# Group ends of the scan: state keys turned behind the second output part, last parts signalled tile by tile, masks moved up

## Chip, cores and metric

The kernel runs on one core of a Trainium2 chip. The metric is the device time of one execution in microseconds. Five engines with queues of their own take part: TensorE (PE, its weight loads PEld), VectorE (DVE), ScalarE (ACT), GpSimd (POOL) and SyncE (SP, which issues the DMAs). They are ordered among each other by semaphores only: an instruction that waits holds up all that stands behind it in its engine's queue.

## What is computed

Six blocks with residual connections work on 1024 tokens (two sequences of 512) of width 512: a gated feed-forward block, a state-space mixer, the feed-forward block again, a routed block, an attention block, and the routed block again. The change is in the mixer. Cut to what matters:

```
proj = rmsnorm(x) @ in_proj_w.T            # gate 8192, hid 8192, B and C 8 x 128 each, dt 128 heads
hid, B, C = silu(causal_conv(hBC))         # 4 taps
M = (C @ B.T) * exp(segsum(A dt))          # inside a chunk, lower triangle
y = M @ (hid dt)  +  C @ state carried from the chunk before  +  Dp * hid
yg = y * silu(gate)
out = rmsnorm over each of 8 groups of 1024 (yg) * gnorm_w @ out_proj_w.T
x = x + out
```

Each of the 8 groups has its own B and C, which its 16 heads share.

## The kernel before

`mamba` (line 1237 on) handles the mixer as a scan over 64 units of two heads (128 columns). Eight units form a group (GT = 8), and there are 8 groups. All large products are done in three passes with operands split into a high and a low part: `matmul3` (lines 73 to 78) issues lo x hi, hi x hi and hi x lo into the same PSUM bank. The high part of a weight tile is made by ScalarE (`split`, L1574), the low part by GpSimd (`low`, L1710).

In a unit TensorE does, in the order of its queue: `states` (L1463, the state of the first chunk, bank 4), `within` for both sequences (L1478 and L1482, banks 5 and 6), `carried` (L1494, bank 7), the transposes of the next unit's hidden columns (`turn`, L1451), and the projections of a later hidden tile and a gate tile into pairs of banks 0 to 3. VectorE does the outputs of these (`skip`, `carried`, `by_token`), the convolution (L1795), the decay differences (L1812) and the `products` of decay and inner products (L1827).

After the eighth unit of a group comes its end, which is where the change lies:

- TensorE projects B and C of the next group, then does the output projection of the group: two output parts p (one for each sequence), each over i = 0 to 7 (`out_part`, called part (p,i) below). A part (p,i) is twelve products: four token tiles t, each accumulated over i in its own bank 4 + t, three passes each. Behind part (0,2) stand the sums of squares (`sums`, L1504). Between part (0,7) and part (1,0) stand the `inner` products of the next group (C B^T for both sequences, L1430 and L1432) and `turn_b` (L1441), which transposes the state keys B of the next group.
- ScalarE makes the high part of the scaled operand (`z_part`, L1646) two parts ahead, and after each part splits the weight tile four ahead (`after_part`). `turned_b` (L1592) copies the transposed keys out of PSUM, ahead of its work for the parts (1,i).
- VectorE makes the operand's low part (`z_low`, L1854), one for each part; after part (p,7) it adds the four finished tiles to x (`outputs`, L1867), each scaled by the reciprocal root of the group's mean square. Between the low parts of sequence 1 it also masks the next group's inner products (`masked`, L1818) and does the products of the next unit (L1827).
- GpSimd makes the low parts of the weights, one for each part, and `rstd` (L1781) behind one of them.

Banks 0 to 3 are two pairs that the users take in turn in the order of `Plan.uses`. A user waits until the one two places ahead in that list has been read: the transposed keys ("bt") share a pair with the inner products of sequence 0 ("cb", grp, 0), so `turn_b` waits for the mask of that sequence; the states of the next unit 8, 16, ... wait for the copied keys and for the first of the four outputs of sequence 1, as bank 4 is used again.

One semaphore `out_used` counts parts; it is raised by the last product of each part. Readers wait for part number + 1: `z_part` before it overwrites an operand buffer, `after_part` before it overwrites a weight buffer, `outputs` once, for part (p,7), before all four tiles.

Of the kernel before, what the change touches and what calls it, by code (L numbers as in the profile page):

```python
# [35 lines left out]
GT = GW // P  # L36
# [1200 lines left out]
def mamba(nc, g, name):  # L1237
# [7 lines left out]
    with ExitStack() as ctx:  # L1245
# [17 lines left out]
        with ExitStack() as pre:  # L1263
# [24 lines left out]

        names = ("const_in", "cw_in", "full", "w_hi", "w_lo", "tapped", "active", "hc_ready", "hcw_ready", "sub_d",
                 "sub_a", "sub_p", "exped", "m_ready", "state", "prev_ready", "y_done", "o_done", "skipped", "yo_ready",  # L1290
                 "combined", "gated", "squared", "added", "rstd_ready", "z_hi", "z_lo", "out_used", "out_read", "dve")
        s = {n: c_.sem(n) for n in names}
        free = [c_.sem(f"free{i}") for i in range(2)]
        raw_in = [c_.sem(f"raw_in{i}") for i in range(NRAW)]
# [26 lines left out]

        def part(grp, p, i):
            return (grp * 2 + p) * GT + i

        with nc.Block() as block:
            @block.sync
# [77 lines left out]
            def _(e):  # L1404
# [103 lines left out]
                def out_part(grp, p, i):  # L1508
                    k, q = plan.tile["o", grp, p, i], part(grp, p, i)
                    e.wait_ge(s["w_lo"], k + 1)  # L1510
                    e.wait_ge(s["z_lo"], q + 1)
                    if i == 0 and p == 0:
                        e.wait_ge(s["skipped"], (grp + 1) * GT)
                        e.wait_ge(s["yo_ready"], (grp + 1) * GT)
                    for t in range(4):
                        if i == 0 and p == 1:
                            e.wait_ge(s["out_read"], 8 * grp + t + 1)
                        sl = (slice(None), q % 2, slice(t * P, (t + 1) * P))
                        last = matmul3(e, ps[4 + t], zs.hi[sl], zs.lo[sl], w.hi[:, k % NSPLIT, :],
                                       w.lo[:, k % NSPLIT, :], i == 0, i == GT - 1)  # L1520
                    last.then_inc(s["out_used"], 1)

                for item in (("B", 0), ("C", 0), ("h", 0), ("h", 1), ("g", 0)):
                    project(item, 0)
# [5 lines left out]
                for u in range(UNITS):  # L1530
                    grp = u // GT
                    more = grp + 1 < GROUPS
                    states(u)
                    within(u, 0)
                    within(u, 1)
                    carried(u)
                    if u + 1 < UNITS:
                        turn(u + 1)
                    for item in (("h", u + 2), ("g", u + 1)):
                        if item[1] < UNITS:  # L1540
                            project(item, 0)
                            project(item, 1)
                    if u % GT < GT - 1:
                        continue
                    if more:
                        for item in (("B", grp + 1), ("C", grp + 1)):
                            project(item, 0)
                            project(item, 1)
                    for i in range(GT):
                        out_part(grp, 0, i)  # L1550
                        if i == 2:
                            sums(grp)
                    if more:
                        inner(grp + 1, 0)
                        inner(grp + 1, 1)
                        turn_b(grp + 1)
                    for i in range(GT):
                        out_part(grp, 1, i)

            @block.scalar  # L1560
            def _(e):
# [79 lines left out]
                def z_part(grp, p, i):  # L1641
                    q = part(grp, p, i)
                    e.wait_ge(s["gated"], grp * GT + i + 1)
                    if q >= 2:
                        e.wait_ge(s["out_used"], q - 1)
                    e.activation(zs.hi[:, q % 2, :], z[:, i, p, :], ACT.Copy, scale=dgn[:, grp, i, 1:2]  # L1646
                                 ).then_inc(s["z_hi"], 1)

                def after_part(grp, p, i):
                    e.wait_ge(s["out_used"], part(grp, p, i) + 1)  # L1650
                    split(plan.tile["o", grp, p, i] + 4)

                for k in range(4):
# [12 lines left out]
                for u in range(UNITS):  # L1666
                    grp, i = divmod(u, GT)
                    more = grp + 1 < GROUPS
                    if u + 1 < UNITS:
                        silu("h", u + 1)  # L1670
                    pass_states(u)
                    if i:
                        gate_silu(u)
                    if u + 1 < UNITS:
                        decay(2 * u + 2)
                        all_differences(2 * u + 3)
                    if u + 2 < UNITS:
                        newest_tap("h", u + 2)
                    if u + 1 < UNITS:
                        decay(2 * u + 3)  # L1680
                    square(u)
                    if i < GT - 1:
                        continue
                    if more:
                        gate_silu(u + 1)
                    z_part(grp, 0, 0)
                    z_part(grp, 0, 1)
                    if more:
                        newest_tap("B", grp + 1)
                        newest_tap("C", grp + 1)  # L1690
                        silu("B", grp + 1)
                    for i in range(GT):
                        z_part(grp, (i + 2) // GT, (i + 2) % GT)
                        after_part(grp, 0, i)
                        if i == 2 and more:
                            silu("C", grp + 1)
                    if more:
                        turned_b(grp + 1)
                    for i in range(GT):
                        if i + 2 < GT:  # L1700
                            z_part(grp, 1, i + 2)
                        after_part(grp, 1, i)

            @block.gpsimd
            def _(e):
# [78 lines left out]
            def _(e):  # L1784
# [75 lines left out]
                                    ).then_inc(free[pair_of("sum", grp)], 1)  # L1860

                def outputs(grp, p):
                    e.wait_ge(s["out_used"], part(grp, p, GT - 1) + 1)
                    e.wait_ge(s["rstd_ready"], grp + 1)
                    for t in range(4):
                        n = p * 4 + t
                        e.scalar_tensor_tensor(x[:, n, :], ps[4 + t], rstd[:, n:n + 1], x[:, n, :], ALU.mult, ALU.add  # L1867
                                               ).then_inc(s["out_read"], 1)

# [12 lines left out]
                for u in range(UNITS):  # L1882
                    grp, i = divmod(u, GT)
# [27 lines left out]
                    z_low(grp, 1, 1)  # L1911
                    if more:
                        masked(grp + 1, 0)
                    z_low(grp, 1, 2)
                    if more:
                        products(2 * u + 2)
                    z_low(grp, 1, 3)
                    if more:
                        masked(grp + 1, 1)
                    z_low(grp, 1, 4)  # L1920
                    if more:
                        products(2 * u + 3)
                    for i in range(5, GT):
                        z_low(grp, 1, i)
                    outputs(grp, 1)

# [243 lines left out]
```

## Time and profile before

| what | value |
|---|---|
| median of 3 runs | 2625.44 us (2620.22 to 2627.13) |
| the profiled execution | 2624.77 us |
| its span | 2622.7 us |
| mean granted TensorE clock | 0.959 |
| PE busy | 2382.1 us, 91% |
| DVE busy | 1674.2 us, 64% |
| ACT busy | 1315.6 us, 50% |
| POOL busy | 1336.2 us, 51% |

A busy share is taken over the whole span. The scan of the mixer takes from about 300 to 1925 us of it. The hardware's records give the start of an instruction well; the end of a matmul is modelled, and neighbouring matmuls overlap in the records, so distances between starts are the better measure on TensorE. On VectorE an instruction's record overlaps the one before it by some 0.1 us. A clock of 1.00 is 2.4 GHz, 0.50 is 1.2 GHz.

### The profile page before, as it was taken

The numbers are of one execution on the slowest core, as the hardware profiler recorded it, in microseconds if no ns is written. First come the engines' busy times: TensorE is split into PE (matmuls) and PEld (weight loads), VectorE is DVE, ScalarE is ACT, GpSimd is POOL, SyncE is SP. The second block draws the span as 40 slices with busy tenths as digits, with TensorE's granted clock in tenths as the row PEclk, the third lists the DMA queues.
The fourth block names the chain that finished last, engine by engine and source line by source line (L and its number), as shares of the span: only waits on it lengthen the run. The fifth ranks groups of instructions, "written<-read, shape, count | busy, mean of one in ns | idle before, by whom it ended". The sixth has DMA issues, their size and how long they took to land. (4 is left out here: it accounts for less than half of the span.)

```text
span 2622.7 us, 32589 instructions
## 1 busy us (share of the span) xinstructions
PE 2382.1 (91%) x12122; PEld 1839.7 (70%) x12122; DVE 1674.2 (64%) x2174; ACT 1315.6 (50%) x1910; POOL 1336.2 (51%) x881
## 2 busy tenths in 40 slices
PE   4995689999999999999999999999759987989986
PEld 4874468778778778878878878878648763565643
DVE  4554478578678678678678678668445534574424
ACT  2321367557557557557657657657423214325533
POOL 1222169669669669759759759759612210000000
PEclk9997799999999999999999999999879997989998
DMA  3430323323323323323323323323114312000001
GB/s 99 107 87 1 95 89 113 96 89 113 97 89 110 97 88 112 96 86 113 97 86 106 103 79 107 109 77 113 52 48 107 96 27 75 1 2 2 2 2 45
DMA packets 163260, 203.97 MB, mean 78 GB/s; under 512 B 24380, under 2 KB 86080, under 8 KB 162976
## 3 DMA queue, kind: packets, MB, share of 16 engines
q1 hardware_dynamic: 163104, 201.90, 26.1%
q8 instruction: 97, 1.59, 0.3%
q14 instruction: 59, 0.48, 0.1%
HBM read 198.37 MB, written 3.15 MB: 77 GB/s over the span
## 5 line engine op out<-in xcount | busy, mean ns | idle before, releaser
L1710 POOL TENSOR_TENSOR mamba_w_lo<-mamba_raw,mamba_w_hi 128x512 fp32r<-128x512 f32 x272 | 435.3, 1610 | 292.8 <-ACT mamba_w_hi L1574 292.8
L76 PE MATMUL psum<-mamba_hT_lo,mamba_w_hi 128*128 128x512 f32 x1152 | 461.7, 401 | 6.5 <-POOL mamba_w_lo L1710 6.5
L78 PE MATMUL psum<-mamba_hT_hi,mamba_w_lo 128*128 128x512 f32 x1152 | 456.0, 396 | 0.0
L77 PE MATMUL psum<-mamba_hT_hi,mamba_w_hi 128*128 128x512 f32 x1152 | 455.9, 396 | 0.0
L1729 POOL TENSOR_SCALAR mamba_L<-mamba_A,mamba_ts 128x256 f32<-128x256 f32 (+1 forms) x256 | 333.3, 1317 | 0.1
L1827 DVE TENSOR_TENSOR mamba_L<-mamba_L,mamba_cb 128x1536 f32<-128x1536 f32 x128 | 309.0, 2414 | 22.5 <-ACT mamba_L L1623 14.2
L1795 DVE SCALAR_TENSOR_TENSOR mamba_hid<-psum,mamba_cw,mamba_hid 128x1022 f32<-128x1022 f32 (+2 forms) x192 | 245.1, 1277 | 21.4 <-ACT mamba_hid L1581 16.8
L76 PEld LDWEIGHTS psum<-mamba_hT_lo,mamba_w_hi 128*128 128x128 f32 x1152 | 216.9, 188 | 56.6 <-POOL mamba_w_lo L1710 6.7
L78 PEld LDWEIGHTS psum<-mamba_hT_hi,mamba_w_lo 128*128 128x128 f32 x1152 | 216.7, 188 | 52.4
L77 PEld LDWEIGHTS psum<-mamba_hT_hi,mamba_w_hi 128*128 128x128 f32 x1152 | 217.1, 188 | 49.1
L350 POOL TENSOR_TENSOR ffn_w_lo<-ffn_deq,ffn_w_hi 128x512 fp32r<-128x512 f32 (+2 forms) x66 | 84.4, 1279 | 296.0 <-ACT ffn_w_hi L360 296.0
L1854 DVE SCALAR_TENSOR_TENSOR mamba_zs_lo<-mamba_z,mamba_dgn,mamba_zs_hi 128x512 fp32r<-128x512 f32 x128 | 117.2, 920 | 175.2 <-ACT mamba_zs_hi L1646 175.2
L1812 DVE SCALAR_TENSOR_TENSOR mamba_L<-mamba_A,mamba_ts,mamba_zero 128x256 f32<-128x256 f32 (+1 forms) x512 | 215.7, 489 | 10.8 <-DMA mamba_A<-mamba_a_dram 10.8
L76 PE MATMUL psum<-mamba_w_lo,mamba_zs_hi 128*128 128x512 f32 x512 | 205.7, 402 | 14.0 <-DVE mamba_zs_lo L1854 13.1
L77 PE MATMUL psum<-mamba_w_hi,mamba_zs_hi 128*128 128x512 f32 x512 | 203.4, 397 | 0.0
L78 PE MATMUL psum<-mamba_w_hi,mamba_zs_lo 128*128 128x512 f32 x512 | 203.3, 397 | 0.0
L1646 ACT ACTIVATE mamba_zs_hi<-mamba_z,mamba_dgn 128x512 fp32r<-128x512 f32 x128 | 91.7, 722 | 192.0 <-PE psum L78 192.0
L1574 ACT CAST mamba_w_hi<-mamba_raw 128x512 fp32r<-128x512 f32 x272 | 165.9, 610 | 36.5 <-PE psum L78 25.8
L489 POOL MEMSET routed_qT<- 1x1024 f32 x2 | 1.9, 945 | 356.3 <-POOLq L53 356.3
L1581 ACT ACTIVATE mamba_hid<-psum,mamba_cw 128x1024 f32<-128x1024 f32 x64 | 77.2, 1206 | 202.0 <-PE psum L78 202.0
L1478 PE MATMUL psum<-mamba_L,mamba_hc 128*64 128x256 f32 x1024 | 159.6, 390 | 3.7 <-DVE mamba_L L1827 3.7
L76 PE MATMUL psum<-ffn_hT_lo,ffn_w_hi 128*128 128x512 f32 (+1 forms) x352 | 139.4, 396 | 23.3 <-POOL ffn_w_lo L350 23.3
(284 smaller groups left out, 4975.1 us busy)
## 6 DMA issues: line engine op xcount, KB each, us to landing
mamba_A<-mamba_a_dram SPq DMA_DIRECT2D x128, 512.0 KB, 4.5
mamba_raw<-in_win SPq DMA_DIRECT2D x144, 256.0 KB, 2.7
mamba_raw<-in_wout SPq DMA_DIRECT2D x128, 256.0 KB, 2.6
mamba_Eb<-mamba_e_dram SPq DMA_DIRECT2D x128, 128.0 KB, 3.0
ffn_raw<-in_w SPq DMA_DIRECT2D x80, 128.0 KB, 3.5
ffn_scl<-in_s SPq DMA_DIRECT2D x80, 128.0 KB, 3.7
ffn_scl<-in_s SPq DMA_DIRECT2D x86, 64.0 KB, 2.4
ffn_raw<-in_w SPq DMA_DIRECT2D x20, 256.0 KB, 2.7
```

The lines of the kernel that those rows point to most:

```text
L76: e.matmul(out, wh, ml, start=start, stop=False)
L77: e.matmul(out, wh, mh, start=False, stop=False)
L78: return e.matmul(out, wl, mh, start=False, stop=stop)
L1478: e.matmul(psum[lo:lo + HD, 5 + b, q:q + HALF], hc[:, token_tile(b, c, 0), lo:lo + HD], L[:, m % 3, c, h, 0:HALF], start=True, stop=False)
L1574: e.copy(w.hi[:, k % NSPLIT, :], raw[:, k % NRAW, :]).then_inc(s["w_hi"], 1)
L1646: e.activation(zs.hi[:, q % 2, :], z[:, i, p, :], ACT.Copy, scale=dgn[:, grp, i, 1:2]).then_inc(s["z_hi"], 1)
L1710: e.tensor_tensor(w.lo[:, k % NSPLIT, :], raw[:, k % NRAW, :], w.hi_read[:, k % NSPLIT, :], ALU.subtract).then_inc(s["w_lo"], 1)
L1729: last = e.tensor_scalar(out, A[:, m % 2, h, lo:SEQ], ts[:, token_tile(b, 1, j), 1, head], 0.0, ALU.subtract, ALU.min)
L1795: ins = e.scalar_tensor_tensor(t[:, :, k:], banks(kind, n)[:, :, :SEQ - k], cw[:, grp, i, 3 - k:4 - k], t[:, :, k:], ALU.mult, ALU.add)
L1812: last = e.scalar_tensor_tensor(out, A[:, m % 2, h, lo:hi], ts[:, token_tile(b, c, j), 1, head], zero[:, 0:1].to_broadcast([P, hi - lo]), ...
L1827: e.tensor_tensor(t, t, cb[:, m % 2].unsqueeze(2).to_broadcast([P, 2, 2, WCOL]), ALU.mult).then_inc(s["m_ready"], 1)
L1854: e.scalar_tensor_tensor(zs.lo[:, q % 2, :], z[:, i, p, :], dgn[:, grp, i, 1:2], zs.hi_read[:, q % 2, :], ALU.mult, ALU.subtract).then_inc ...
```

## The change

- `turn_b` of the next group leaves its place ahead of part (1,0) and stands behind part (1,1); ScalarE's `turned_b` likewise stands behind its work for part (1,1).
- The last part of each sequence, (p,7), raises a new semaphore `out_done` four times, once for each finished token tile, and no longer `out_used`, which now counts seven parts for each sequence. A function `taken` gives for a part number the semaphore and the value to wait for. `outputs` waits for each tile by itself instead of once for all four.
- VectorE's order behind part (0,7): before it was low part (1,1), mask 0, low part (1,2), products of the next unit's sequence 0, low part (1,3), mask 1, low part (1,4), products of its sequence 1, low parts (1,5) to (1,7). Now it is low part (1,1), mask 0, products of sequence 0, mask 1, low part (1,2), products of sequence 1, low parts (1,3) to (1,7).

```diff
--- before.py
+++ after.py
@@ -1288,7 +1288,7 @@
 
         names = ("const_in", "cw_in", "full", "w_hi", "w_lo", "tapped", "active", "hc_ready", "hcw_ready", "sub_d",
                  "sub_a", "sub_p", "exped", "m_ready", "state", "prev_ready", "y_done", "o_done", "skipped", "yo_ready",
-                 "combined", "gated", "squared", "added", "rstd_ready", "z_hi", "z_lo", "out_used", "out_read", "dve")
+                 "combined", "gated", "squared", "added", "rstd_ready", "z_hi", "z_lo", "out_used", "out_done", "out_read", "dve")
         s = {n: c_.sem(n) for n in names}
         free = [c_.sem(f"free{i}") for i in range(2)]
         raw_in = [c_.sem(f"raw_in{i}") for i in range(NRAW)]
@@ -1321,6 +1321,11 @@
 
         def part(grp, p, i):
             return (grp * 2 + p) * GT + i
+
+        def taken(q):
+
+            n, i = divmod(q, GT)
+            return (s["out_done"], 4 * (n + 1)) if i == GT - 1 else (s["out_used"], n * (GT - 1) + i + 1)
 
         with nc.Block() as block:
             @block.sync
@@ -1518,7 +1523,10 @@
                         sl = (slice(None), q % 2, slice(t * P, (t + 1) * P))
                         last = matmul3(e, ps[4 + t], zs.hi[sl], zs.lo[sl], w.hi[:, k % NSPLIT, :],
                                        w.lo[:, k % NSPLIT, :], i == 0, i == GT - 1)
-                    last.then_inc(s["out_used"], 1)
+                        if i == GT - 1:
+                            last.then_inc(s["out_done"], 1)
+                    if i < GT - 1:
+                        last.then_inc(s["out_used"], 1)
 
                 for item in (("B", 0), ("C", 0), ("h", 0), ("h", 1), ("g", 0)):
                     project(item, 0)
@@ -1553,9 +1561,10 @@
                     if more:
                         inner(grp + 1, 0)
                         inner(grp + 1, 1)
-                        turn_b(grp + 1)
                     for i in range(GT):
                         out_part(grp, 1, i)
+                        if more and i == 1:
+                            turn_b(grp + 1)
 
             @block.scalar
             def _(e):
@@ -1642,12 +1651,12 @@
                     q = part(grp, p, i)
                     e.wait_ge(s["gated"], grp * GT + i + 1)
                     if q >= 2:
-                        e.wait_ge(s["out_used"], q - 1)
+                        e.wait_ge(*taken(q - 2))
                     e.activation(zs.hi[:, q % 2, :], z[:, i, p, :], ACT.Copy, scale=dgn[:, grp, i, 1:2]
                                  ).then_inc(s["z_hi"], 1)
 
                 def after_part(grp, p, i):
-                    e.wait_ge(s["out_used"], part(grp, p, i) + 1)
+                    e.wait_ge(*taken(part(grp, p, i)))
                     split(plan.tile["o", grp, p, i] + 4)
 
                 for k in range(4):
@@ -1694,12 +1703,12 @@
                         after_part(grp, 0, i)
                         if i == 2 and more:
                             silu("C", grp + 1)
-                    if more:
-                        turned_b(grp + 1)
                     for i in range(GT):
                         if i + 2 < GT:
                             z_part(grp, 1, i + 2)
                         after_part(grp, 1, i)
+                        if more and i == 1:
+                            turned_b(grp + 1)
 
             @block.gpsimd
             def _(e):
@@ -1860,10 +1869,10 @@
                                     ).then_inc(free[pair_of("sum", grp)], 1)
 
                 def outputs(grp, p):
-                    e.wait_ge(s["out_used"], part(grp, p, GT - 1) + 1)
                     e.wait_ge(s["rstd_ready"], grp + 1)
                     for t in range(4):
                         n = p * 4 + t
+                        e.wait_ge(s["out_done"], 8 * grp + n + 1)
                         e.scalar_tensor_tensor(x[:, n, :], ps[4 + t], rstd[:, n:n + 1], x[:, n, :], ALU.mult, ALU.add
                                                ).then_inc(s["out_read"], 1)
 
@@ -1911,16 +1920,13 @@
                     z_low(grp, 1, 1)
                     if more:
                         masked(grp + 1, 0)
+                    if more:
+                        products(2 * u + 2)
+                        masked(grp + 1, 1)
                     z_low(grp, 1, 2)
                     if more:
-                        products(2 * u + 2)
-                    z_low(grp, 1, 3)
-                    if more:
-                        masked(grp + 1, 1)
-                    z_low(grp, 1, 4)
-                    if more:
                         products(2 * u + 3)
-                    for i in range(5, GT):
+                    for i in range(3, GT):
                         z_low(grp, 1, i)
                     outputs(grp, 1)
```

## Rows read from the trace of the kernel before

**Rows 1.** Cores: span and mean granted TensorE clock.
```profile
core 0: 2622.7 us, clock 0.959
```

**Rows 2.** Windows: length, busy time of PE, PEld, DVE, ACT, POOL, clock, DMA.
```profile
343.00:510.00 167.00, 166.94 (x939) 135.13 (x940) 129.63 (x141) 114.11 (x148) 139.34 (x88) 0.99 0.35 106
510.00:546.00 36.00, 32.70 (x153) 26.03 (x153) 19.94 (x21) 13.96 (x24) 16.26 (x12) 1.00 0.28 81
```

**Rows 3.** Waits of TensorE: in total, times, the longest.
```profile
PE psum L76 <- DVE mamba_zs_lo L1854: 13.1, 8, 8.7
...
PE psum L1441 <- DVE mamba_cb L1818: 12.1, 7, 1.7
...
PE psum L1463 <- DVE s_x L1867: 6.5, 7, 0.9
```

**Rows 4.** Timeline, TensorE: start, length, instruction, idle before; ahead of part (1,0).
```profile
517.40 0.38 PE L1432 MATMUL psum<-mamba_bc 128*128 128x128 f32 x2
519.51 0.66 PE L1441 MATMUL psum<-s_ident,mamba_bc 128*128 128x128 f32 x4 [1.73 <-DVE mamba_cb L1818]
519.92 0.51 PE L76 MATMUL psum<-mamba_w_lo,mamba_zs_hi 128*128 128x512 f32 x1
```

**Rows 5.** Timeline, VectorE, first group end.
```profile
515.21 2.73 DVE L1867 SCALAR_TENSOR_TENSOR s_x<-psum,mamba_rstd,s_x 128x512 f32<-128x512 f32 x4 [1.23 <-PE psum L78]
517.85 0.74 DVE L1854 SCALAR_TENSOR_TENSOR mamba_zs_lo<-mamba_z,mamba_dgn,mamba_zs_hi 128x512 fp32r<-128x512 f32 x1
518.51 0.95 DVE L1818 TENSOR_TENSOR mamba_cb<-psum,mamba_mask 128x768 f32<-128x768 f32 x1
...
524.52 2.85 DVE L1827 TENSOR_TENSOR mamba_L<-mamba_L,mamba_cb 128x1536 f32<-128x1536 f32 x1
527.30 1.79 DVE L1854 SCALAR_TENSOR_TENSOR mamba_zs_lo<-mamba_z,mamba_dgn,mamba_zs_hi 128x512 fp32r<-128x512 f32 x1
```

**Rows 6.** Timeline, TensorE, from part (1,2) to part (1,3).
```profile
528.21 0.39 PE L78 MATMUL psum<-mamba_w_hi,mamba_zs_lo 128*128 128x512 f32 x1
529.24 0.47 PE L76 MATMUL psum<-mamba_w_lo,mamba_zs_hi 128*128 128x512 f32 x1 [0.64 <-DVE mamba_zs_lo L1854]
```

**Rows 7.** Timeline, TensorE: end of part (1,7), and the next unit.
```profile
543.08 0.40 PE L78 MATMUL psum<-mamba_w_hi,mamba_zs_lo 128*128 128x512 f32 x1
544.41 1.13 PE L1463 MATMUL psum<-mamba_hcw,mamba_bt 128*128 128x128 f32 x8 [0.94 <-DVE s_x L1867]
...
547.90 0.39 PE L1482 MATMUL psum<-mamba_L,mamba_hc 128*64 128x128 f32 x4
548.22 1.13 PE L1494 MATMUL psum<-mamba_bc,mamba_prev 128*128 128x256 f32 x4
...
561.03 0.40 PE L78 MATMUL psum<-mamba_hT_hi,mamba_w_lo 128*128 128x512 f32 x1
561.26 0.94 PE L1463 MATMUL psum<-mamba_hcw,mamba_bt 128*128 128x128 f32 x7
```

**Rows 8.** Timeline, GpSimd, first group end.
```profile
516.57 1.27 POOL L1710 TENSOR_TENSOR mamba_w_lo<-mamba_raw,mamba_w_hi 128x512 fp32r<-128x512 f32 x1 [1.45 <-ACT mamba_w_hi L1574]
524.41 1.35 POOL L1710 TENSOR_TENSOR mamba_w_lo<-mamba_raw,mamba_w_hi 128x512 fp32r<-128x512 f32 x1 [6.56 <-ACT mamba_w_hi L1574]
```

**Rows 9.** Lines of products and low parts: shortest, median, longest in ns.
```profile
L1827 DVE TENSOR_TENSOR mamba_L<-mamba_L,mamba_cb x128: 1757/2404/3018, 336.3 to 1854.4; 128x1536 f32<-128x1536 f32 x128
...
L1854 DVE SCALAR_TENSOR_TENSOR mamba_zs_lo<-mamba_z,mamba_dgn,mamba_zs_hi x128: 735/751/2346, 482.2 to 1917.0; 128x512 fp32r<-128x512 f32 x128
```

**Rows 10.** Timeline, ScalarE: high part of (1,2).
```profile
523.10 0.72 ACT L1646 ACTIVATE mamba_zs_hi<-mamba_z,mamba_dgn 128x512 fp32r<-128x512 f32 x1 [2.31 <-PE psum L78]
```

**Rows 11.** Timeline, TensorE and VectorE, end of the last group.
```profile
1899.04 0.47 PE L76 MATMUL psum<-mamba_w_lo,mamba_zs_hi 128*128 128x512 f32 x1 [0.94 <-DVE s_x L1867]
...
1921.72 2.73 DVE L1867 SCALAR_TENSOR_TENSOR s_x<-psum,mamba_rstd,s_x 128x512 f32<-128x512 f32 x4 [4.01 <-PE psum L78]
1925.45 4.85 DVE L137 BATCH_NORM_STATS2 ffn_n_st<-s_x 128x6 f32<-128x512 f32 x8 [1.00 <-PEq L53]
```

## The prediction

> **What bounds the kernel now.** I read the totals first, then the table of who waited for whom, then three stretches of the timeline around the end of one group of the scan. The profiled execution has a span of 2622.7 us [rows 1] and took 2624.77 us, so 2.07 us lie outside the span; it stands 0.67 us under the median of the runs, 2625.44 us. The table by stretches shows what sets the pace in the scan: from 343 to 510 us TensorE is busy for 166.94 of 167.00 us at a granted clock of 0.99, that is at its 2.4 GHz level, while VectorE has 129.63 and GpSimd 139.34; from 510 to 546, the end of the first group, TensorE has only 32.70 of 36 [rows 2]. So between group ends nothing but TensorE counts, and each microsecond in which it stands still at a group end is a microsecond of the kernel. The table of waits names what stops it there: the mask (L1818) before the transposes of the state keys, 12.1 us in seven times; the output of the gated sum (L1867) before the states, 6.5 in seven; the low part of the output operand (L1854), 13.1 in eight, of which one is an 8.7 us wait at the last group that this change does not touch, so seven share about 4.4 [rows 3]. That is (12.1 + 6.5 + 4.4) / 7 = 3.3 us idle for each of the seven group ends that have a successor.
>
> **Where the three stops lie (first group end).** I measure from start to start, since the modelled ends of matmuls overlap by some 0.17 us.
> A: the last inner product starts at 517.40, the transposes at 519.51, the first product of output part (1,0) at 519.92: 2.52 us [rows 4]. The transposes cannot start before the mask of sequence 0 has freed their two PSUM banks, and VectorE does that mask only after four outputs (2.73 us) and a low part [rows 5].
> B: the last product of part (1,2) starts at 528.21, the first of part (1,3) at 529.24 [rows 6]. The pitch of such products is 0.23 (561.03 to 561.26 [rows 7]), so 0.80 is lost. VectorE had put products (2.85 us) between the low parts of (1,2) and (1,3), and the latter itself took 1.79 [rows 5].
> C: the last product of part (1,7) starts at 543.08, the states at 544.41, 1.33 us later; one unit on, where nothing stands between, it is 561.03 to 561.26, 0.23 [rows 7]. So 1.10 is lost waiting for the first of four outputs, which starts only when all four tiles of the part are finished.
>
> **The change, part by part.**
> *Transposes behind part (1,1), their copy in ScalarE's queue likewise.* TensorE goes from the inner products to part (1,0) without asking for a mask. The switch costs something like the one from L1482 to L1494, 547.90 to 548.22, 0.32 us [rows 7]. A shrinks from 2.52 to 0.32: part (1,0) starts 2.20 earlier, at S = 517.72. The other conditions of that part are met: its low operand is written at 513.98 (VectorE's idle time of 1.23 before the outputs at 515.21 begins there [rows 5]), and its first tile needs only the first output. The bounds of the switch are 0.23 (no cost beyond the pitch) and 0.41 (519.51 to 519.92, in which four transposes go by as well [rows 4]); I take 0.32, since it too goes from 128-column products to wider ones. The four transposes are not removed: in the new place they cost 519.92 - 519.51 = 0.41, and the restart after them 0.12 (by the stretch 519.92 to 528.21, 36 products at 0.23 and 0.2 over), 0.53 in all. What ScalarE's copy of the 512 columns delays there: the queue behind it is the high part of (1,4), which waits for the end of part (1,2) anyway, over 2 us later; the weights of (1,1) are split before it. It also no longer holds ScalarE ahead of part (1,2). Nothing is taken from or given to SP's queue, and GpSimd's order is the same; the weight loads follow the parts.
> *Masks and products moved up.* This decides whether B goes. I lay VectorE's new order out against the rows. Part (0,7) still ends at 515.21; its tiles of three products (0.70 us each) are finished at 513.11, 513.81, 514.51 and 515.21. VectorE is free at 513.98, so the four outputs run with their present pitch of 2.64 / 4 = 0.66 and the next instruction starts at 516.62 instead of 517.85. Then low part (1,1) to 517.28, mask 0 to 518.23, products(16) with up to 2.85 to 521.1, mask 1 to 522.0. If GpSimd is idle, which it is from 517.84 until the split after part (1,0) [rows 8], products(16) take their shortest 1.76 [rows 9], and the second mask ends at 520.9. Low part (1,2) needs its high part, which follows the end of part (1,0): 523.10 - 519.92 + 0.72 = 3.90 after S [rows 4, 10], that is 521.62. So VectorE is back in time, the low part runs to 522.4, and part (1,2) wants it at S + 2 x 2.84 + 0.53 = 523.93 (2.84 is a part: (528.21 + 0.23 - 519.92) / 3). From here the distances to S are those of before: products start at S + 4.60, beside the same GpSimd split, and part (1,3) can start at 529.24 - 519.92 = S + 9.32. TensorE asks for it at S + 8.52 + 0.53 = S + 9.05. So the stall B is not removed by the move: its 0.80 is filled with the transposes, and 0.27 remains. A and B together give exactly the 2.20 by which S comes earlier, with bounds of 2.11 (the switch at its dear end) and 2.29 + 0.27 = 2.56 (cheap switch, no stall left). Behind (1,3) VectorE has only low parts left, so it is not late again.
> *Last parts signal tile by tile.* In part (1,7) the first tile is finished 2.10 before the last, VectorE has nothing else to do (4.01 idle ahead of the same outputs in the last group [rows 11]), and the first output of 0.74 is over 1.2 us before the states want bank 4. The second, third and fourth end at most 0.74 after the last tile, while the carried product asks for the fourth 3.8 us after the states begin (548.22 - 544.41 [rows 7]). C falls to 0.23: 1.10 saved; bounds 0 and 1.10. In the last group the same wait stands before part (1,0) (0.94 idle at 1899.04 [rows 11]) and goes for the same reason: 1.10. At the very end the four outputs start at 1921.72 and take 2.73, and the statistics of the next stage follow them after 1.00 [rows 11]; with tiles signalled singly only the fourth is left behind the last product: 2.73 - 0.74 = 1.99 saved, all on the path, because TensorE waits for VectorE there.
> *Signals.* Sixteen last parts carry four signals instead of one, and VectorE four waits instead of one. The row bound is zero: the last product of a projection, at 561.03, carries a signal too, and the next one starts the plain 0.23 behind it [rows 7]. The Trainium skill, page "TensorE: Matmul & The Clock Gate", section "The cost: per-tile semaphore tail", speaks against this change: increments on completion serialize at about 26 ns each. By that rule 48 more increments are an estimated 1.2 us; the sum would be 25.0 instead of 26.2. No run here shows it, and I do not count it.
> *The shared port.* That a low part or a products instruction stretches beside a GpSimd subtraction is in the rows: products take 2.85 against a shortest 1.76, with GpSimd's 1.35 us instruction started 0.11 before them [rows 5, 8, 9]; the outputs, which read PSUM, run at 0.74 each through the whole of GpSimd's 516.57 instruction. No row has a mask beside GpSimd; I take it like an output, as it also reads PSUM, with 1.29 (a whole GpSimd instruction) as the other end, of which the 0.7 us between 520.9 and 521.62 takes half and the rest is the first rival's way. The Trainium skill, page "SBUF — State Buffer", section "Who interferes with whom", has this as an exclusive lock; by its rule for one SBUF input the mask would not be held, which leaves the sum as it is.
>
> **Sum.** 7 x 2.20 + 7 x 1.10 + 1.10 + 1.99 = 15.4 + 7.7 + 1.1 + 2.0 = 26.2 us. Against the profiled execution 2624.8 - 26.2 = 2598.6; against the median 2599.2. I say 2599.
>
> **Rivals.**
> 1. *VectorE is late for low part (1,2) by one lock.* Products(16), low part (1,1) or a mask meet GpSimd's subtraction at 516.57 or take 2.85 rather than 1.76, the whole row slides, and products(17) start later. If VectorE gains nothing from the single signals (low part (1,1) at 517.85 and mask 0 at 518.51 as today), low part (1,2) starts at 518.51 + 0.95 + 2.85 + 0.95 less the small overlaps of neighbours, about 523.1 instead of 521.66, and part (1,3) slides by the same 1.45: 7 x 1.45 = 10.2 given back, 2609. For it: low part (1,1) at 516.62 and GpSimd at 516.57 nearly coincide. Against it: one such meeting costs at most 1.3, and between 520.9 and 521.62 only the rest counts.
> 2. *The states stay held.* Another condition, the rest of the outputs or ScalarE's queue, replaces C: 7.7 lost, 2607. Against: the distances of 1.2 and 3.8 us above.
> 3. *Slower than before.* The moved masks and products now stand before low part (1,2), and if each meeting with GpSimd is at its dearest, TensorE waits twice. With the longest low part of the trace, 2.35, and the longest products, 3.02 [rows 9]: 516.62 + 2.35 + 0.95 + 3.02 + 0.95 + 2.35 = 526.2; then 3.02 + 2.35 more, and part (1,3) starts at 531.8, S + 14.0 instead of S + 9.3. That is 4.7 a group against 3.3 saved: +1.4 x 7 - 3.1 = +6.7, 2632. It decides from S + 13.1 on. Against it: the extreme rows come from elsewhere in the scan (here products are 2.85 at most), and GpSimd has but one instruction for each part.
> 4. *The signals do not do what they say*, because TensorE's tiles finish no earlier than the part does for VectorE: C and the end stay, 15.4 is left, 2610.
>
> **Chances.** Forecast 0.75, first rival 0.12, second 0.04, fourth 0.03, slower 0.03, the rest 0.03. The range goes from the full 2.56 a group and some of the spread of the runs below their median (26.2 + 2.5 + 4 off 2625.4) to the first rival: 2593 to 2610. What a measurement can tell is 0.3%, 7.9 us: faster than 2617.6 0.93, within 0.04, slower 0.03; all rivals but the third are faster by more.
>
> **What would show it.** No wait of L1441 for the mask; L1463 without a wait for L1867 at seven places; the step from the last inner product to part (1,0) near 0.3; transposes of 0.4 inside part (1,1)'s end; a wait of at most 0.3 for L1854 at part (1,3); the period from one group's transposes to the next 3.3 us shorter; VectorE's last output ending one output behind TensorE. I am wrong if L76 waits longer than 1 us for L1854 in a group, if a wait for anything new stands before L1463, or if the units between group ends, now with no idle time, get longer.

## The result and the profile after

The changed kernel takes 2591.28 us (median of 4 runs, 2589.62 to 2592.27) against 2625.72 (4 runs, 2620.22 to 2627.13): a ratio of 0.9869, 95% interval 0.9854 to 0.9883, or 34.4 us less. Forecast were 26.2 us and 2599, with a range that ended at 2593.

TensorE's waits in the changed kernel, that answer to [rows 3]:

```profile
PE psum L76 <- DVE mamba_zs_lo L1863: 10.0, 8, 8.7
...
PE psum L1468 <- ACT mamba_bt L1601: 5.7, 1, 5.7
```

Line numbers are 5 to 9 higher than before (the states are L1468, the transposes L1446, the low part L1863, the outputs L1876). The mask and the outputs are gone from the list. Of the 10.0 us for low parts, 8.7 are the last group's, unchanged, and seven waits share 1.3. The wait for the copied keys is the one at the very start of the scan.

TensorE's timeline at the first group end (start, length, instruction, idle before), that answers to [rows 4, 6, 7] (a row with x2 or x4 stands for so many instructions in a row, with the start of the first):

```profile
521.29 0.38 PE L1437 MATMUL psum<-mamba_bc 128*128 128x128 f32 x2
521.43 0.48 PE L76 MATMUL psum<-mamba_w_lo,mamba_zs_hi 128*128 128x512 f32 x1
521.75 0.39 PE L77 MATMUL psum<-mamba_w_hi,mamba_zs_hi 128*128 128x512 f32 x1
521.98 0.39 PE L78 MATMUL psum<-mamba_w_hi,mamba_zs_lo 128*128 128x512 f32 x1
...
526.88 0.40 PE L78 MATMUL psum<-mamba_w_hi,mamba_zs_lo 128*128 128x512 f32 x1
527.12 0.60 PE L1446 MATMUL psum<-s_ident,mamba_bc 128*128 128x128 f32 x4
527.48 0.48 PE L76 MATMUL psum<-mamba_w_lo,mamba_zs_hi 128*128 128x512 f32 x1
...
530.12 0.39 PE L78 MATMUL psum<-mamba_w_hi,mamba_zs_lo 128*128 128x512 f32 x1
530.70 0.47 PE L76 MATMUL psum<-mamba_w_lo,mamba_zs_hi 128*128 128x512 f32 x1 [0.19 <-DVE mamba_zs_lo L1863]
...
544.55 0.39 PE L78 MATMUL psum<-mamba_w_hi,mamba_zs_lo 128*128 128x512 f32 x1
544.78 1.05 PE L1468 MATMUL psum<-mamba_hcw,mamba_bt 128*128 128x128 f32 x8
```

From the start of the last two inner products to part (1,0) it is 0.14 us instead of 2.52. The transposes take 0.36 at their new place behind part (1,1), and the product behind them is followed by the next 0.31 us later instead of 0.23: 0.44 in all. Part (1,3) begins 9.27 us after part (1,0), against 9.32 before: still held by the low part, for 0.35 beyond the pitch (0.58 from start to start) instead of 0.80. The states follow part (1,7) at the plain pitch of 0.23. The other six group ends repeat these distances within 0.02 us.

VectorE over the same stretch, that answers to [rows 5]:

```profile
517.78 2.72 DVE L1876 SCALAR_TENSOR_TENSOR s_x<-psum,mamba_rstd,s_x 128x512 f32<-128x512 f32 x4
520.41 0.74 DVE L1863 SCALAR_TENSOR_TENSOR mamba_zs_lo<-mamba_z,mamba_dgn,mamba_zs_hi 128x512 fp32r<-128x512 f32 x1
521.07 0.95 DVE L1827 TENSOR_TENSOR mamba_cb<-psum,mamba_mask 128x768 f32<-128x768 f32 x1
522.13 1.79 DVE L1836 TENSOR_TENSOR mamba_L<-mamba_L,mamba_cb 128x1536 f32<-128x1536 f32 x1
523.84 0.94 DVE L1827 TENSOR_TENSOR mamba_cb<-psum,mamba_mask 128x768 f32<-128x768 f32 x1
525.34 0.75 DVE L1863 SCALAR_TENSOR_TENSOR mamba_zs_lo<-mamba_z,mamba_dgn,mamba_zs_hi 128x512 fp32r<-128x512 f32 x1 [0.55 <-ACT mamba_zs_hi L1655]
526.00 2.85 DVE L1836 TENSOR_TENSOR mamba_L<-mamba_L,mamba_cb 128x1536 f32<-128x1536 f32 x1
528.77 1.78 DVE L1863 SCALAR_TENSOR_TENSOR mamba_zs_lo<-mamba_z,mamba_dgn,mamba_zs_hi 128x512 fp32r<-128x512 f32 x1
```

and GpSimd beside it, that answers to [rows 8]:

```profile
520.46 1.84 POOL L1719 TENSOR_TENSOR mamba_w_lo<-mamba_raw,mamba_w_hi 128x512 fp32r<-128x512 f32 x1 [1.45 <-ACT mamba_w_hi L1583]
525.88 1.35 POOL L1719 TENSOR_TENSOR mamba_w_lo<-mamba_raw,mamba_w_hi 128x512 fp32r<-128x512 f32 x1 [3.58 <-ACT mamba_w_hi L1583]
528.69 1.31 POOL L1719 TENSOR_TENSOR mamba_w_lo<-mamba_raw,mamba_w_hi 128x512 fp32r<-128x512 f32 x1 [1.46 <-ACT mamba_w_hi L1583]
```

The outputs run straight behind low part (1,0), VectorE is back 0.55 us before low part (1,2) can start, and then the old pattern returns: products of 2.85 behind GpSimd's instruction at 525.88, low part (1,3) of 1.78 behind the one at 528.69.

**Where the 34.4 us are.** To see what belongs to the group ends and what does not, I cut every trace at five starts of TensorE: the inner products of sequence 1 for the first group (335.36 us in the kernel before), the last unit's states (1851.45), the scan's last product (1921.28), the first transpose of the next stage (1933.53) and the program's last product (2612.46). "Step" is the stretch from the third to the fourth, "behind" that from the fourth to the fifth. In us, one profiled execution each, and the median of the timed runs:

```
kernel            start   7 group ends'  last    step to     behind   median
                  at      part of scan   group   next stage
before            335.4   1516.1         69.8    12.25       678.9    2625.7
before, again     339.2   1515.8         69.9    12.24       673.5    2623.1
masks alone       336.0   1516.5         68.2    12.23       672.3    2625.1
turn alone        335.8   1499.7         70.0    12.23       675.3    2606.9
turn and masks    336.1   1503.2         69.7    12.24       675.0    2610.9
signals alone     335.3   1498.4         68.8    10.26       678.9    2601.5
turn and signals  335.5   1491.3         67.5    10.26       678.1    2592.5
changed           339.3   1491.2         67.1    10.26       672.1    2591.3
changed, again    337.8   1490.9         67.3    10.26       672.2    2592.0
end at once       335.3   1490.9         68.3    12.30       672.2    2598.6
shift by two      335.9   1491.0         67.2    11.57       676.5    2593.9
shift by four     336.9   1490.6         66.9    12.89       678.3    2599.1
products later    338.7   1488.0         66.9    10.27       671.9    2588.3
```

The second column repeats within 0.4 us for one kernel. The change takes 24.9 us there (forecast 23.1), 2.7 in the last group (1.1), 1.99 in the step (1.99): 29.6 us. The other 4.8 of 34.4 come from no stretch in which a line was changed. In the profiled pair such stretches give 3.0: 6.9 less behind the scan, 3.9 lost ahead of it (the start at 335.4 or 339.2 in the two profiles of the kernel before, 339.3 and 337.8 in those of the changed one). The last 1.9 are the difference between the medians, 34.4, and the profiled executions, 2624.8 - 2592.3 = 32.5. A profiled execution can lie well off its median (masks alone 2618.7, end at once 2591.8), so what an edit does is read from the columns by stretch, and the medians only confirm it.

### The profile page after: what moved, and what is told of

Same layout as the page of the kernel before. It is cut to its first block and busy times, and to the rows that moved or that the text cites. A ratio compares the mean times of both kernels' runs of the same rounds, so it can differ in the third digit from the quotient of the medians.

```text
span 2590.2 us, 32589 instructions
## 1 busy us (share of the span) xinstructions
PE 2371.8 (92%) x12122; PEld 1835.4 (71%) x12122; DVE 1668.5 (64%) x2174; ACT 1314.4 (51%) x1910; POOL 1336.1 (52%) x881
## 5 line engine op out<-in xcount | busy, mean ns | idle before, releaser
L1836 DVE TENSOR_TENSOR mamba_L<-mamba_L,mamba_cb 128x1536 f32<-128x1536 f32 x128 | 301.9, 2359 | 23.1 <-ACT mamba_L L1632 14.2
L1863 DVE SCALAR_TENSOR_TENSOR mamba_zs_lo<-mamba_z,mamba_dgn,mamba_zs_hi 128x512 fp32r<-128x512 f32 x128 | 117.5, 923 | 171.8 <-ACT mamba_zs_hi L1655 171.8
```

What stands on the lines that cost most here:

```text
L1836: e.tensor_tensor(t, t, cb[:, m % 2].unsqueeze(2).to_broadcast([P, 2, 2, WCOL]), ALU.mult).then_inc(s["m_ready"], 1)
L1863: e.scalar_tensor_tensor(zs.lo[:, q % 2, :], z[:, i, p, :], dgn[:, grp, i, 1:2], zs.hi_read[:, q % 2, :], ALU.mult, ALU.subtract).then_inc ...
```

## The experiments

**1. The changed kernel again**, no edit.

> The changed kernel once more, nothing edited. Theory: the scan gives the same 27 to 28 us in every execution (24.9 at the seven group ends, about 3 at the last), and what the profiled pair shows outside the scan (4.4 us lost ahead of it, 8.8 won behind it) is where TensorE's half-rate stretches happen to fall; then the distance from the last group's end to the end of the program differs from the 714.0 us of the first profile of this kernel by 1 us or more, and the ratio stays within 0.985 to 0.990. Rival: the 8.8 us behind the scan belong to the change; then that distance repeats within 0.5 us and lies 8 to 9 us below that of every profile of the kernel before.

Measured: 2592.02 us (2591.24 to 2592.13), ratio 0.9884 [0.9868, 0.9899]. The stretch behind the scan is 672.2, so the rival's first half held: it repeats.

**2. The kernel before again**, no edit.

> The kernel before once more, nothing edited. Theory (half-rate stretches fall differently from run to run): its stretch behind the scan moves by more than 1 us against its own first profile, and total half-rate time is not 219 us again. Rival (the 8.8 us belong to the change): it repeats within 0.5 us. Ratio 1.000 within 0.002 under both.

Measured: 2623.08 us (2617.65 to 2628.64, 11 runs), ratio 1.0004 [0.9994, 1.0015]. Behind the scan 673.5 instead of 678.9: here the theory held. So neither was wholly right: this stretch takes 672 to 673.5 in some executions of either kernel, and 679 in one of the old.

**3. The transposes alone** behind part (1,1).

```diff
                         inner(grp + 1, 1)
-                        turn_b(grp + 1)
                     for i in range(GT):
                         out_part(grp, 1, i)
+                        if more and i == 1:
+                            turn_b(grp + 1)
...
-                    if more:
-                        turned_b(grp + 1)
                     for i in range(GT):
                         if i + 2 < GT:
                             z_part(grp, 1, i + 2)
                         after_part(grp, 1, i)
+                        if more and i == 1:
+                            turned_b(grp + 1)
```

> Only the transposes and their copy behind part (1,1); signals and VectorE's order as before. Theory: part (1,0) starts 0.14 behind the last inner product instead of 2.52, part (1,3) is held to its old distance of 9.3 from there, so 7 x 2.38 = 16.7 us, about 2609, and the 1.33 before the states stays. Rival (masks in their old place reach the transposes too late): TensorE waits for the mask behind part (1,1) and under 10 us are saved.

Measured: 2606.89 us (2598.61 to 2610.73), ratio 0.9938 [0.9920, 0.9957]. The seven group ends give 16.4 us (2.3 each); the waits of L1463 for the outputs stay at 6.6 us in seven. As the theory had it.

**4. The signals alone**: the new semaphore, `taken` and the wait for each tile, orders as before.

> Only the tile-by-tile signals; transposes and VectorE's order as before. Theory: the four outputs end 1.2 us earlier, so the mask does too and the wait before the transposes falls from 1.73 to about 0.5; with 1.10 before the states 7 x 2.3 + 1.1 + 2.0 = 19.2 us, about 2606. Together with the transposes alone this is more than the whole change, by the 7 x 1.2 that both save at the same wait. Rival (each edit saves waits of its own): only 7 x 1.1 + 3.1 = 10.8 us, about 2615.

Measured: 2601.45 us (2595.26 to 2606.23), ratio 0.9919 [0.9901, 0.9936]. The seven ends give 17.7 us, 2.5 each against the 2.3 expected, so the theory held and its rival (1.1 each) did not. This is the line in which the signals' hidden share stands, the mask's wait before the transposes (12.1 us before):

```profile
PE psum L1446 <- DVE mamba_cb L1826: 2.9, 7, 0.4
```

Single signals let VectorE reach the mask 1.3 us sooner. Alone, transposes and signals give 16.4 + 17.7 = 34.1, together (experiment 7) 24.8: at seven ends 9.3 us are the same wait, counted twice.

**5. VectorE's order alone.**

```diff
                         masked(grp + 1, 0)
+                    if more:
+                        products(2 * u + 2)
+                        masked(grp + 1, 1)
                     z_low(grp, 1, 2)
                     if more:
-                        products(2 * u + 2)
-                    z_low(grp, 1, 3)
-                    if more:
-                        masked(grp + 1, 1)
-                    z_low(grp, 1, 4)
-                    if more:
                         products(2 * u + 3)
-                    for i in range(5, GT):
+                    for i in range(3, GT):
                         z_low(grp, 1, i)
```

> Only VectorE's new order of masks and products; transposes and signals as before. Theory: mask 0 stays where it is, so the wait before the transposes stays at 1.73, and low part (1,2) is still followed by products, so the 0.62 before part (1,3) stays too: no change, 2624. Rival (it is the moved masks that fill the stall before (1,3)): 7 x 0.8 = 5.6 us less, 2618.

Measured: 2625.14 us (2618.09 to 2628.41, 12 runs), ratio 0.9997 [0.9984, 1.0009]. No change, and none at the seven ends (1516.5 against 1516.1 and 1515.8).

**6. Transposes and order, no signals.**

> The whole change without the tile-by-tile signals. Theory: low part (1,1) starts 1.2 later, so the second mask ends at about S + 4.5 and low part (1,2) meets GpSimd's split there; products and low part (1,3) slide, part (1,3) starts about 0.7 us later than with the transposes alone: 2607 + 5 = 2612 (this is the first rival of the prediction, in the kernel where VectorE gains nothing from the signals). Rival (the new order is at least harmless): 2607 or less, like the transposes alone.

Measured: 2610.86 us (2608.24 to 2613.99), ratio 0.9952 [0.9937, 0.9967]; the seven ends are 3.5 us longer than with the transposes alone. VectorE in this kernel, then GpSimd:

```profile
522.21 0.95 DVE L1819 TENSOR_TENSOR mamba_cb<-psum,mamba_mask 128x768 f32<-128x768 f32 x1
523.08 1.72 DVE L1855 SCALAR_TENSOR_TENSOR mamba_zs_lo<-mamba_z,mamba_dgn,mamba_zs_hi 128x512 fp32r<-128x512 f32 x1
524.72 1.75 DVE L1828 TENSOR_TENSOR mamba_L<-mamba_L,mamba_cb 128x1536 f32<-128x1536 f32 x1
526.39 1.77 DVE L1855 SCALAR_TENSOR_TENSOR mamba_zs_lo<-mamba_z,mamba_dgn,mamba_zs_hi 128x512 fp32r<-128x512 f32 x1
```

```profile
522.97 1.28 POOL L1711 TENSOR_TENSOR mamba_w_lo<-mamba_raw,mamba_w_hi 128x512 fp32r<-128x512 f32 x1 [4.14 <-ACT mamba_w_hi L1575]
525.77 1.84 POOL L1711 TENSOR_TENSOR mamba_w_lo<-mamba_raw,mamba_w_hi 128x512 fp32r<-128x512 f32 x1 [1.52 <-ACT mamba_w_hi L1575]
```

Here the second mask ends too late, GpSimd starts 0.11 us before low part (1,2), which takes 1.72 instead of 0.75, and everything behind it slides (part (1,2) begins 6.43 us behind part (1,0) instead of 6.05, part (1,3) 9.80 instead of 9.27): the first rival, at a third of the price I gave it (0.5 us a group, not 1.45), because the products then run free at 1.75.

**7. Transposes and signals, VectorE's order as before.**

> The whole change with VectorE's order as before. Theory: everything that was gained comes from the transposes and the signals; low part (1,2), products, low part (1,3) follow each other as in the kernel before, 9.3 us after S: scan 1558 us, time 2591 to 2593, the same as the whole change. Rival (the moved masks and products pay): 3 us or more above it.

Measured: 2592.49 us (2589.39 to 2595.0), ratio 0.9880 [0.9864, 0.9897]; the seven ends 1491.3 against 1491.2 for the whole change. Beside the other two edits, the moved masks and products give nothing.

**8. The changed kernel with the second products behind low part (1,3).**

```diff
                     z_low(grp, 1, 2)
+                    z_low(grp, 1, 3)
                     if more:
                         products(2 * u + 3)
-                    for i in range(3, GT):
+                    for i in range(4, GT):
```

> The changed kernel with the second products instruction moved from behind low part (1,2) to behind low part (1,3). Theory: low part (1,3) is ready before TensorE asks, the 0.35 us at part (1,3) (0.58 from start to start against 0.23) goes at seven ends: scan 2.4 us shorter than 1558.2, time 2589; products then end before low part (1,4) is wanted. Rival (the stall moves): products and GpSimd's split stand before low part (1,4), TensorE waits there for 0.4 or more, no gain or 2593.

Measured: 2588.28 us (2586.56 to 2589.04), ratio 0.9864 [0.9846, 0.9881]; every run of it is below every run of the changed kernel. The seven ends are 3.1 us shorter, a little more than the 7 x 0.35 expected: each gives 0.35 at the stop and 0.07 behind it, since part (1,3), when it begins after a stop, takes 2.87 or 2.88 us and otherwise 2.80. VectorE, with both low parts at 0.75 now:

```profile
524.68 0.75 DVE L1863 SCALAR_TENSOR_TENSOR mamba_zs_lo<-mamba_z,mamba_dgn,mamba_zs_hi 128x512 fp32r<-128x512 f32 x1 [0.55 <-ACT mamba_zs_hi L1655]
527.49 0.75 DVE L1863 SCALAR_TENSOR_TENSOR mamba_zs_lo<-mamba_z,mamba_dgn,mamba_zs_hi 128x512 fp32r<-128x512 f32 x1 [2.05 <-ACT mamba_zs_hi L1655]
528.15 2.85 DVE L1836 TENSOR_TENSOR mamba_L<-mamba_L,mamba_cb 128x1536 f32<-128x1536 f32 x1
530.93 0.74 DVE L1863 SCALAR_TENSOR_TENSOR mamba_zs_lo<-mamba_z,mamba_dgn,mamba_zs_hi 128x512 fp32r<-128x512 f32 x1
```

The one wait of TensorE left for a low part is the last group's. This is the best version found.

**9. The last group's outputs at once**: `outputs` waits for `out_done` at 8 x 7 + 4p + 4 first when the group is the last.

> The changed kernel, but in the last group both outputs wait until all four tiles are finished, as before the change. Theory: only the last group and the step behind it grow, by 1.1 (the wait before part (1,0), 0.94 idle) and 2.0 (10.26 to 12.25 us from the scan's last product to the next stage's first): 3.1 us on the 1591.3 or so of scan and step; of the time 2 to 9 us, since the stretch behind it can fall into either of the lengths seen, 672 or 675 to 679. Rival (the step is set by something else than the last outputs): 0.

Measured: the step is 12.30 instead of 10.26 and the last group 68.3 instead of 67.2, 3.1 us as the theory had it; the time is 2598.61 us (2591.77 to 2601.34), ratio 0.9896 [0.9878, 0.9914]. That is 6.6 to 7.3 over the changed kernel's medians, in the expected 2 to 9; but this run and the next two were timed on another chip than experiment 1, where the kernel before stood at 2626.3 beside them against 2623.7 beside experiment 1. By the ratios it is 3.1 us over experiment 1 and 7.1 over the first measurement. The profiled execution was the fastest of its runs.

**10 and 11. A pure delay behind the scan**: two or four more low parts behind the last outputs, written to the unused gate buffer.

```diff
                     outputs(grp, 1)
+                    if not more:
+                        for k in range(2):      # or 4
+                            e.scalar_tensor_tensor(gate[:, k // 2, k % 2, :], z[:, 0, 0, :], ...)
```

> The changed kernel with two more low parts (VectorE, 0.66 us each from start to start, into a buffer that nobody reads) behind the last outputs of the scan: a pure delay of 1.3 us between the scan and the stretch behind it. Theory (where TensorE's half-rate stretches fall depends on the moment at which the stages behind the scan begin): the stretch behind the scan changes its length by more than 1 us, so the time moves by clearly more or less than 1.3. Rival (its length belongs to the kernel's edits): 672.2 again and 1.3 us more in the time, 2593.

> As above with four, a pure delay of 2.6 us. Theory: the stretch behind the scan has another length than 672.2, by 1 us or more; the time lies anywhere from 2590 to 2601. Rival: 672.2 again, and 2594.5.

Measured: 2593.85 us (2589.16 to 2594.52), ratio 0.9878 [0.9860, 0.9897], and 2599.06 us (2595.53 to 2599.71), ratio 0.9901 [0.9885, 0.9916]. The steps are 11.57 and 12.89, the delays 1.3 and 2.6 as meant; behind them 676.5 and 678.3 instead of 672.2. The rival's 672.2 did not come in either profile. The times are weaker evidence than the profiles: the median of the shorter delay, 2593.9, cannot tell the two apart, and the longer one stands 7 to 8 us over the changed kernel's medians, but only 4.5 over experiment 1 by the ratios, whose intervals overlap.

## Why the prediction was wrong

The direction, the places and the order of the terms held; the sum was 8.2 us short, which put the time 1.7 us under the range. By the prediction's own steps:

- *A and the transposes.* "I take 0.32" for the switch from the inner products to part (1,0) was the wrong row: it measured 0.14, below even the bound of 0.23 "no cost beyond the pitch". Measured like the 2.52, from the start of the last two inner products, these 0.14 hold 0.11 from the one to the other and 0.03 to part (1,0), where the first pitch is then 0.32 (521.43 to 521.75) instead of 0.23. S, the start of part (1,0), came 2.38 earlier, not 2.20. The transposes and their restart cost 0.44 of the 0.53 given.
- *B.* As laid out: the stall is not removed but filled; 9.27 us from part (1,0) to part (1,3) against a forecast 9.32. What is left of the stop, 0.35, was given as 0.27. S and B together give 7 x (0.18 + 0.05) = 7 x 0.23 = 1.6 of the 1.8 us that the seven ends gave beyond the forecast.
- *Masks and products moved up* "decides whether B goes", I wrote. It decides nothing: experiments 5 and 7 show 0 alone and 0 with the rest, and experiment 6 shows it harmful without the signals. My layout did contain this (the distances behind low part (1,2) are those of before), but I did not draw it.
- *C and the last group's wait.* 1.10 each, right: 0.23 stands where 1.33 stood, and experiment 9 puts the last group's 1.1 back.
- *The end.* 1.99, right to the hundredth (12.25 to 10.26).
- *Signals.* No cost seen: in part (1,7), which now carries four signals, the products keep their pitch of 0.23, and so do the states behind them (544.55 to 544.78). The 1.2 us that the prediction worked out from the Trainium skill, page "TensorE: Matmul & The Clock Gate", section "The cost: per-tile semaphore tail", did not show. That section gives its figure for the tail behind the last product; whether there is such a tail here, hidden behind the products that follow, no run tells.
- *The shared port.* Right: mask 0 ran at 0.95 through GpSimd's instruction at 520.46, while low part (1,1), started 0.05 before that instruction, held it up to 1.84. The Trainium skill, page "SBUF — State Buffer", section "Who interferes with whom", calls this an exclusive lock and exempts a VectorE instruction with at most one SBUF input outside the 2-port modes; these rows agree with both. That low part (1,1) and GpSimd "nearly coincide" was the first rival's argument; VectorE was first here.
- *The third rival's sum.* Its terms add up to 531.6 and not 531.8, so about 2631 and not 2632; nothing hangs on it.

**The step that failed** is one I did not write down as a step: the sum has four terms and takes the rest at nothing, as if no stretch outside the changed waits could change its length. The 8.2 us by which it fell short are 1.8 at the seven ends, 1.6 in the last group beyond its 1.1, and 4.8 that no changed stretch holds (3.0 outside the scan in the profiled pair, the rest the difference between medians and profiled executions). The 1.8 alone would have left 2597.4, inside the range, whose lower end took the full 2.56 a group and 4 us for the spread of runs; the other 6.4, which no term held, took the time out of it. The windows show the last group's. Length, busy times of PE, PEld, DVE, ACT, POOL, granted clock and DMA, over 20 us around the two long waits of the last unit; in the kernel before:

```profile
1855.00:1875.00 20.00, 8.76 (x29) 5.99 (x30) 7.44 (x5) 6.41 (x8) 13.02 (x7) 0.53 0.08 26
```

in the changed kernel:

```profile
1834.00:1854.00 20.00, 8.71 (x32) 6.25 (x33) 7.49 (x5) 6.41 (x8) 13.06 (x7) 0.66 0.09 26
```

and with VectorE's order alone, where this stretch is the code of before:

```profile
1856.00:1876.00 20.00, 8.69 (x33) 6.19 (x34) 7.43 (x5) 6.41 (x8) 13.10 (x7) 0.66 0.09 26
```

TensorE is granted its 1.2 GHz level nearly throughout (0.53) or with a piece of 2.4 GHz between (0.66), and the last group takes 69.8 or 68.2 us for it with no change in its instructions. So 1.6 of the 2.7 us are the clock. The 13 profiles bear it out. Over the whole last group the clock is 0.85 in five of them and 0.90 in eight. With one signal for a sequence it lasts 69.7 to 70.0 us at 0.85 and 68.2 at 0.90; tile by tile it lasts 68.8 at 0.85 and 66.9 to 67.5 at 0.90 (68.3 where experiment 9 makes it wait again). The same holds behind the scan, here over 5 us some 147 us behind the start of the next stage, in the kernel before:

```profile
2081.00:2086.00 5.00, 4.57 (x13) 3.62 (x14) 4.93 (x11) 0.18 (x1) 1.28 (x1) 0.66 0.11 26
```

in the changed kernel:

```profile
2055.00:2060.00 5.00, 4.80 (x21) 3.90 (x22) 4.93 (x11) 0.00 (x0) 1.29 (x1) 1.00 0.17 54
```

and with VectorE's order alone:

```profile
2080.40:2085.40 5.00, 5.00 (x22) 4.03 (x23) 4.75 (x10) 0.00 (x0) 1.09 (x1) 1.00 0.22 64
```

A piece at half clock is there or not, and 13 products pass in these 5 us, or 21 to 22. Several such pieces make the 672 to 679 us: summed from the trace's clock records, TensorE stands at 1.2 GHz for 110 of the 679 us in the kernel before and for 89 of the 672 in the changed one. In all 13 profiles the clock of this stretch is 0.92 where it took 676.5 us or more and 0.93 where it took 675.4 or less. That both lengths occur without any change in the code is shown (the two profiles of before, and experiment 5). That the moment at which the stages begin bears on it is shown only so far that a delay of 1.3 and 2.6 us came with 4.3 and 6.1 more behind it, in one profile each; against a simple rule stands experiment 9, whose profile has 2.0 us delay and still 672.2. Why the changed kernel found 672 in both profiles and kept its eight runs within 2.7 us, while the same scan with the old order of VectorE had 678.1 and spreads over 5.6, stays open. Of the 34.4 us I count 28 as the change's own (24.9 + 1.1 + 2.0) and the rest as this.

The timed runs agree. Of the 53 runs of the kernel before whose clock is on record beside the experiments, the 15 with a mean granted clock of 0.962 or more took 2617.5 to 2623.7 us, median 2619.0; the 30 at 0.959 or less took 2621.8 to 2629.8. The changed kernel had 0.962 or more in seven of its eight runs, with a median of 2591.5. At like clocks the two are 27.5 us apart.

## What to carry to other kernels

Lay the queues out in time against the rows, and ask of each moved instruction whether the distance to the next stall is changed: the new order of VectorE looked like the core of the change and moved no distance. Two edits that shorten the same wait must not be added; run each alone and the sum tells the overlap. Where TensorE's clock changes level outside the edited stretch, give the range a few microseconds both ways for it, and compare stretches between fixed landmarks before the totals.

## What was not expected of the hardware

- The same 2,614 products behind the scan took 671.9 to 678.9 us, with the granted clock at 1.2 GHz for 89 to 110 us of it. With a pure delay of 2.6 us ahead of them they took 678.3, with one of 1.3 us 676.5, with none 672.1 and 672.2; but with experiment 9's 2.0 us also 672.2.
- A switch from products of 128 columns to products of 512 costs TensorE little: the first wide one starts 0.03 us behind the last narrow one, and the next 0.32 behind it instead of 0.23. Four transposes take 0.36 from start to start, and the restart behind them 0.08.
- A stop of TensorE costs more than the wait: behind one of 0.35 us, the part that follows takes 0.07 longer.
